# Four places for the routed rows, their loads behind ScalarE's copies, the row weight on y, and copies on POOL

## The reference

```python
masked_scores = sg.reshape(T, E)
_, selected_experts = jax.lax.top_k(masked_scores, K)
weights = jnp.take_along_axis(original_scores, selected_experts, axis=-1)
weights = weights / jnp.sum(weights, axis=-1, keepdims=True)
...
g = jax.lax.ragged_dot(xs, w_gate, group_sizes)     # xs: rows sorted by expert
u = jax.lax.ragged_dot(xs, w_up, group_sizes)
d = jax.lax.ragged_dot(jax.nn.silu(g) * u, w_down, group_sizes)
unsort_idx = jnp.argsort(sort_idx)
out = d[unsort_idx].reshape(T, K, H)
expert_out = jnp.sum(out * weights[..., None], axis=1)
shared = jax.nn.silu(x @ sw_gate) * (x @ sw_up) @ sw_down
return (expert_out + shared).reshape(B, S, H)
```

## Time and profile before

| | us |
|---|---|
| median of 3 runs | 2272.18 |
| lowest, highest | 2271.74, 2274.15 |
| the profiled execution | 2276.63 |
| its span, first to last instruction | 2274.9 |

### The profile page before, as it was taken

How to read it: one execution, slowest core, us unless ns; L and a number is a source line. 1 busy time by engine, 2 the same in 40 slices (tenths; PEclk the granted TensorE clock), 3 DMA queues, 4 the chain that set the end, 5 groups by cost and what they waited for, 6 DMA issues and landing times. The chain is left out here.

```text
span 2274.9 us, 34385 instructions
## 1 busy us (share of the span) xinstructions
PE 1932.6 (85%) x10056; PEld 1382.9 (61%) x10057; DVE 1309.4 (58%) x2357; ACT 573.1 (25%) x1164; POOL 1119.3 (49%) x552
## 2 busy tenths in 40 slices
PE   5956887868887589998799999999999999997891
PEld 3423443743333233343499988888888888886781
DVE  2564543556776767775674446666666666654540
ACT  3320222401114244453222212222222222221210
POOL 0000000002557365664035567666667788877886
PEclk8977998898996789999899999999999999998996
DMA  3043101402224456721125445556555656654999
GB/s 117 0 118 100 52 22 32 172 18 88 80 87 160 153 195 224 233 69 44 40 82 180 180 139 169 160 170 174 159 157 153 196 160 189 193 156 129 209 210 212
DMA packets 272640, 306.01 MB, mean 135 GB/s; under 512 B 40857, under 2 KB 184217, under 8 KB 272569
## 3 DMA queue, kind: packets, MB, share of 16 engines
q1 hardware_dynamic: 142776, 187.24, 25.6%
q10 hardware_dynamic: 108288, 66.88, 11.1%
q0 software_dynamic: 21504, 50.93, 9.5%
HBM read 186.42 MB, written 118.55 MB: 134 GB/s over the span
## 5 line engine op out<-in xcount | busy, mean ns | idle before, releaser
L2495 PE MATMUL psum<-e_gu_high,e_rowT_high 128*128 (+1 forms) x1272 | 435.0, 344 | 43.9 <-issue 19.9
L2495 PE MATMUL psum<-e_gu_low,e_rowT_high 128*128 (+1 forms) x1272 | 410.5, 324 | 0.0
L2495 PEld LDWEIGHTS psum<-e_gu_high,e_rowT_high 128*128 128x128 f32 x1272 | 241.5, 190 | 88.8 <-issue 86.4
L2295 DVE TENSOR_TENSOR e_midT_low<-psum,e_midT_high 128x256 fp32r<-128x256 f32 x159 | 67.5, 424 | 348.8 <-ACT e_midT_high L2209 326.9
L2500 PE MATMUL psum<-e_gu_high,e_rowT_low 128*128 (+1 forms) x1272 | 257.7, 325 | 0.0
L2495 PEld LDWEIGHTS psum<-e_gu_low,e_rowT_high 128*128 128x128 f32 x1272 | 242.6, 191 | 2.2
L2203 ACT CAST e_rowT_high<-psum 128x512 fp32r<-128x512 f32 x127 | 74.6, 587 | 596.4 <-issue 407.9
L2500 PEld LDWEIGHTS psum<-e_gu_high,e_rowT_low 128*128 128x128 f32 x1272 | 215.2, 190 | 0.0
L2515 PE MATMUL psum<-e_d_high,e_midT_high 128*128 (+3 forms) x477 | 190.7, 400 | 3.6 <-ACT e_midT_high L2209 2.4
L2515 PE MATMUL psum<-e_d_low,e_midT_high 128*128 (+3 forms) x477 | 188.3, 395 | 0.0
L2119 POOL TENSOR_TENSOR e_gu_high<-f_gu_in,e_ones 128x1408 fp32r<-128x1408 f32 x31 | 78.6, 2535 | 182.1 <-PE psum L2500 161.4
(11 more groups left out here) (381 smaller groups left out, 3941.3 us busy)
## 6 DMA issues: line engine op xcount, KB each, us to landing
d_sorted<-f_hs SPq DMA_DIRECT2D x32, 1048.0 KB, 10.3
d_y<-f_arena ACTq DMA_DIRECT2D x127, 256.0 KB
e_row<-d_sorted ACTq DMA_DIRECT2D x500, 64.0 KB
f_gu_in<-in_L_ffn_w_gate SPq DMA_DIRECT2D x32, 704.0 KB
f_gu_in<-in_L_ffn_w_up SPq DMA_DIRECT2D x32, 704.0 KB, 6.1
f_d_in<-in_L_ffn_w_down SPq DMA_DIRECT2D x32, 512.0 KB
d_y<-f_hs SPq DMA_DIRECT2D x8, 1024.0 KB, 5.7
f_d_in<-in_L_ffn_w_down SPq DMA_DIRECT2D x32, 192.0 KB
```

Source lines behind the costliest of these rows:

```text
L2495: nc.tensor.matmul(bank[:, 0:M].unsqueeze(1), rowT_high[par][:, k, :], w[:, bass.ds(buffer, 1), k, at:at + M], start=(k == 0 and n == 0), ...
```

## The change

There are four places for routed rows instead of two, and they lie in the first four tiles of `hs`, which are free once their rows have been scattered and turned. SP fills four places before the loop. ScalarE issues the loads of tile i+4 after `copy_midT`, ahead of the store of y, behind waits for the pick and the transpose of tile i. On DVE the transpose of tile i+1 moves from the end of step i-1 to the start of step i, behind the copy of y; rowT's low part then comes ahead of midT's; the pick for tile i moves from step i-1 to the place behind the product of tile i; the product no longer takes the row weight; y is multiplied by it on its way out of PSUM. The loops of ScalarE and DVE hold four tiles instead of two; PE's program stays as it is. On POOL the four products with ones become `tensor_copy`.

```diff
-        row = [sbuf(nc, stack, f"e_row{n}", [P, D]) for n in range(2)]
-        side = [sbuf(nc, stack, f"e_side{n}", [P, 2 * TOPK]) for n in range(2)]
+        row = [hs[:, n, 0:D] for n in range(ROWS)]
+        side = [hs[:, n, D:ROW] for n in range(ROWS)]
         picked = [sbuf(nc, stack, f"e_picked{n}", [P, TOPK]) for n in range(2)]
-        row_weight = [sbuf(nc, stack, f"e_row_weight{n}", [P, 1]) for n in range(2)]
+        row_weight = [sbuf(nc, stack, f"e_row_weight{n}", [P, 1]) for n in range(ROWS)]
...
+        QUAD_END = (TILES - 1 - ROWS) // ROWS
+        def load_row(eng, tile, place):
 
             for r in range(P // BLOCK):
-                eng.dma_start(row[par][r * BLOCK:(r + 1) * BLOCK, :].rearrange("b (n q) -> b n q", n=P // BLOCK).unsqueeze(1),
-                              sorted_blocks[:, tile, :, r * P:(r + 1) * P]).then_inc(row_loaded[par], 16)
-            eng.dma_start(side[par][:].unsqueeze(1), sorted_tiles[:, tile, D:ROW]).then_inc(row_loaded[par], 16)
+                eng.dma_start(row[place][r * BLOCK:(r + 1) * BLOCK, :].rearrange("b (n q) -> b n q", n=P // BLOCK).unsqueeze(1),
+                              sorted_blocks[:, tile, :, r * P:(r + 1) * P]).then_inc(row_loaded[place], 16)
+            eng.dma_start(side[place].unsqueeze(1), sorted_tiles[:, tile, D:ROW]).then_inc(row_loaded[place], 16)
 
...
-            for par in range(2):
-                load_row(sp, slice(par, par + 1), par)
+            sp.wait_ge(row_turned, NT + ROWS)
+            for n in range(ROWS):
+                load_row(sp, slice(n, n + 1), n)
...
-                nc.gpsimd.tensor_tensor(d_high[:, par, 0:2, :], d_in[:, 0:2, :], ones[:, 0:1].unsqueeze(2).broadcast_to((P, 2, D)), ALU.mult)
-                nc.gpsimd.tensor_tensor(d_high[0:LAST_M, par, 2, :], d_in[0:LAST_M, 2, :], ones[0:LAST_M, 0:1].broadcast_to((LAST_M, D)), ALU.mult).then_inc(high_ready, 1)
+                nc.gpsimd.tensor_copy(d_high[:, par, 0:2, :], d_in[:, 0:2, :])
+                nc.gpsimd.tensor_copy(d_high[0:LAST_M, par, 2, :], d_in[0:LAST_M, 2, :]).then_inc(high_ready, 1)
...
-                nc.gpsimd.tensor_tensor(gu_high[:, par, :, 0:M], gu_in[:, :, 0:M], ones[:, 0:1].unsqueeze(2).broadcast_to((P, CC, M)), ALU.mult).then_inc(high_ready, 1)
+                nc.gpsimd.tensor_copy(gu_high[:, par, :, 0:M], gu_in[:, :, 0:M]).then_inc(high_ready, 1)
...
-                nc.gpsimd.tensor_tensor(gu_high[:, par, :, M:2 * M], gu_in[:, :, M:2 * M], ones[:, 0:1].unsqueeze(2).broadcast_to((P, CC, M)), ALU.mult).then_inc(high_ready, 1)
+                nc.gpsimd.tensor_copy(gu_high[:, par, :, M:2 * M], gu_in[:, :, M:2 * M]).then_inc(high_ready, 1)
...
-            def load(i, par):
+            def load(i, place):
                 act.wait_ge(weight_taken, i - SHARED_TILES + 1)
                 act.wait_ge(blocks_turned, i - SHARED_TILES + 1)
-                load_row(act, bass.ds(i + 2 - SHARED_TILES, 1), par)
+                load_row(act, bass.ds(i + ROWS - SHARED_TILES, 1), place)
 
...
-            def steps(i, par, loads=False, stores=False, old=True, more=True, blocks=True):
-                if loads:
-                    load(i, par)
-                if more and blocks:
-                    copy_blocks(i + 1, 1 - par)
+            def steps(i, par, old=True, more=True):
                 silus(i, par)
                 if old:
                     copy_midT(i - 1)
-                if more and not blocks:
+                if more:
                     copy_rowT(i + 1, 1 - par)
+            def routed_steps(i, place, fills, loads=True, stores=True, more=True):
+                par = place % 2
+                if more:
+                    copy_blocks(i + 1, 1 - par)
+                silus(i, par)
+                copy_midT(i - 1)
+                if loads:
+                    load(i, place)
                 if stores:
                     store(i - 2, par)
 
...
-            for i in range(SHARED_TILES, SHARED_TILES + 2):
-                steps(i, i % 2, loads=True)
-            with act.Fori(SHARED_TILES // 2 + 1, LOOP_END) as n:
-                for par in range(2):
-                    steps(n * 2 + par, par, loads=True, stores=True)
-            for i in range(LOOP_END * 2, TILES):
-                steps(i, i % 2, loads=(i + 2 < TILES), stores=True, more=(i + 1 < TILES))
+            for i in range(SHARED_TILES, SHARED_TILES + ROWS):
+                routed_steps(i, i % ROWS, (i + 1 - SHARED_TILES) // ROWS + 1, stores=(i >= SHARED_TILES + 2))
+            with act.Fori(SHARED_TILES // ROWS + 1, QUAD_END) as n:
+                for q in range(ROWS):
+                    routed_steps(n * ROWS + q, q, n + ((q + 1) // ROWS + 1 - SHARED_TILES // ROWS))
+            for i in range(QUAD_END * ROWS, TILES):
+                routed_steps(i, i % ROWS, (i + 1 - SHARED_TILES) // ROWS + 1, loads=(i + ROWS < TILES), more=(i + 1 < TILES))
...
-            def turn_blocks(i, par, loads):
+            def turn_blocks(i, place, loads):
                 dve.wait_ge(rowT_low_ready, i)
-                dve.wait_ge(row_loaded[par], LANDED * loads)
+                dve.wait_ge(row_loaded[place], LANDED * loads)
                 nc.vector.transpose(XT.rearrange("p (n k b) -> p n k b", k=CC, b=BLOCK),
-                                    row[par][:].rearrange("p (n b k) -> p n k b", k=CC, b=BLOCK)).then_inc(blocks_turned, 1)
+                                    row[place].rearrange("p (n b k) -> p n k b", k=CC, b=BLOCK)).then_inc(blocks_turned, 1)
 
...
-            def take_weight(i, par):
+            def take_weight(i, place):
 
                 expert = tile_expert[:, bass.ds(i - SHARED_TILES, 1)]
-                nc.vector.scalar_tensor_tensor(picked[par][:], side[par][:, TOPK:2 * TOPK], expert, side[par][:, 0:TOPK],
-                                               ALU.is_equal, ALU.mult, accum_out=row_weight[par][:]).then_inc(weight_taken, 1)
+                nc.vector.scalar_tensor_tensor(picked[place % 2][:], side[place][:, TOPK:2 * TOPK], expert, side[place][:, 0:TOPK],
+                                               ALU.is_equal, ALU.mult, accum_out=row_weight[place][:]).then_inc(weight_taken, 1)
 
...
-            def multiply(i, par, taken=None):
+            def multiply(i, par):
                 dve.wait_ge(silu_ready, i + 1)
                 dve.wait_ge(up_done, i + 1)
-                if taken is None:
-                    nc.vector.tensor_tensor(mid[par][:], silu[par][:], U[par][:, 0:M], ALU.mult).then_inc(mid_ready, 1)
-                else:
-                    dve.wait_ge(weight_taken, taken)
-                    nc.vector.scalar_tensor_tensor(mid[par][:], silu[par][:], row_weight[par][:], U[par][:, 0:M],
-                                                   ALU.mult, ALU.mult).then_inc(mid_ready, 1)
-
-            def copy_y(i, par, stored=None):
+                nc.vector.tensor_tensor(mid[par][:], silu[par][:], U[par][:, 0:M], ALU.mult).then_inc(mid_ready, 1)
+            def copy_y(i, place, stored=None):
+                par = place % 2
                 dve.wait_ge(down_done, i + 1)
+                dve.wait_ge(weight_taken, i - SHARED_TILES + 1)
                 if stored is not None:
 
                     dve.wait_ge(y_stored[par], stored)
-                nc.vector.tensor_copy(y[par][:], Y[par]).then_inc(y_copied, 1)
+                nc.vector.tensor_scalar(y[par][:], Y[par], row_weight[place][:], None, ALU.mult).then_inc(y_copied, 1)
 
...
-            def routed_steps(i, par, more=True, loads=None):
+            def routed_steps(i, place, fills, more=True):
+                par = place % 2
+                if more:
+                    turn_blocks(i + 1, (place + 1) % ROWS, fills)
+                    low_blocks(i + 1, 1 - par)
                 low_midT(i - 1)
-                if more:
-                    low_blocks(i + 1, 1 - par)
-                    take_weight(i + 1, 1 - par)
-                multiply(i, par, i - SHARED_TILES + 1)
-                if loads is not None:
-                    turn_blocks(i + 2, par, loads)
+                multiply(i, par)
+                take_weight(i, place)
 
...
-            take_weight(SHARED_TILES, 0)
-            turn_blocks(SHARED_TILES + 1, 1, 1)
-            routed_steps(SHARED_TILES, 0, loads=2)
+            routed_steps(SHARED_TILES, 0, 1)
             add_y(SHARED_TILES - 1, 1)
-            for i in range(SHARED_TILES + 1, SHARED_TILES + 4):
-                routed_steps(i, i % 2, loads=(i - SHARED_TILES) // 2 + 2)
-                copy_y(i - 1, (i - 1) % 2, 16 if i == SHARED_TILES + 3 else None)
-            with dve.Fori(SHARED_TILES // 2 + 2, LOOP_END) as n:
-                for par in range(2):
-                    routed_steps(n * 2 + par, par, loads=n - SHARED_TILES // 2 + 2)
-                    copy_y(n * 2 + par - 1, 1 - par, 16 * (n - SHARED_TILES // 2 - 1 + par))
-            for i in range(LOOP_END * 2, TILES):
```

(13 more changed lines are left out.)

14 lines of the change are left out of this document (7 added, 7 removed).

## The result

| kernel | time, us (median; lowest to highest) | span of the profiled execution, us |
|---|---|---|
| before | 2273.16 (2271.74 to 2275.50) | 2274.9 |
| after | 2310.48 (2310.15 to 2310.84) | 2308.9 |

The ratio after to before is 1.0157, 95% interval 1.0145 to 1.0169: the change makes the kernel slower by 1.6%. The profiled execution of after took 2310.68 us. The forecast was 2294 us: the direction is right, and 2310.5 lies inside the likeliest case's own range (2277 to 2312), near its upper end.

What follows compares the result with a forecast made beforehand. PE's routed stage was taken as nearly a matmul stream, losing when another engine is late. Loop +31, first routed tile -2.8, end -9.8 and +3 made +21.4 on 2276.63, 2298.0; less 4.45 for the median, 2294 us, range 2250 to 2335.

Steps and rivals of the forecast that it cites:

- likeliest case: The forecaster's own case, a slower kernel at 2294 us, range 2277 to 2312; chance 0.46.
- nearly equal bounds of 2.01 and 2.03: ScalarE's cast: earliest start in us of a tile, 2.01 by the load issues behind a free pick, 2.03 by the turn.
- The loop: Routed tiles up to POOL's first gather: about +1.0 to +1.2 us per split, times 27 splits, +31 us.
- two worked cases: Four tiles over two splits: 27.82 us with the split in an odd tile (26.69 before), 27.44 in an even one (26.6).
- The undisturbed pair: Two loop tiles without a waiting pick: 6.35 us even plus 6.79 odd, 13.14 together, 6.57 per tile.
- T + 3.05: ScalarE's next cast can't start before the pick's end T plus 0.17, 2.43 and 0.45 us for loads and store.
- POOL's copies: On POOL, copies replacing 2.5 us products take 1.3 us for 1408 elements; a whole split gets 3.7 us shorter.
- (b): Rival: POOL copies no faster than products, +1.95 us a split, +53 in the loop, 2325 us; chance 0.22.
- First routed tile: The turn comes before the pick, so PE's down product starts at 1351.1 instead of 1353.90: -2.8 us.
- The end: POOL's chain from first gather to PE's waiting gate: -9.8 us; afterwards, with PE and POOL level, +3 us.
- (a): Rival: the move is a gain, the pick's wait stays off the path or ScalarE isn't held; 2255 us, chance 0.25.
- (c): Rival: picks mostly wait behind only one low part, excess near 0.65 us per split, gains cancel it; 2272 us, chance 0.07.

Runs made afterwards that it cites:

- fastest kernel: Changed kernel with the turn at the end of DVE's step, loads of the tile before, PE's loop of four and the pick's weights read from PSUM: 2232.7 us.
- pick from PSUM: Changed kernel, but DVE first copies the row's six weights to PSUM and the pick reads them there: 2276.8 us.
- turn at the end: Changed kernel with the transpose back behind the pick at the end of DVE's step, one tile further ahead: 2311.8 us.
- later loads: Changed kernel, but ScalarE's step issues the loads that hang on the pick of the tile before: 2267.3 us.
- products back: Changed kernel with POOL's four products by ones put back in place of the copies: 2382.2 us.
- copies only: Kernel before with POOL's four products by ones replaced by copies, nothing else: 2292.5 us.
- body of four tiles: Changed kernel with the loads of the tile before and PE's loop body holding four tiles instead of two: 2260.9 us.
- products and later loads: Changed kernel with POOL's products by ones put back and with the loads of the tile before: 2298.2 us.

## Why the prediction was right, and which of its terms were off

**The mechanism stands.** Of the signs named ahead, these are in the rows: load issues near 5.4 us of a tile, odd tiles lengthened with the copy at 3.30, a pick that waits over 1.5 us and a tile over 8 us behind it where a split starts in an odd tile, copies near 1.3 us, PE's idle time at "issue". One failed: the cast does come before 2.0, at 1.37, in the even tile that follows a long one, since the long tile gives the engines behind PE their slack back; and behind the 14 even splits the held tile is 7.6 to 7.85, not over 8, as it is behind the 13 odd ones (8.2 to 8.7). The mechanism is more than an argument now: taking the loads from behind the current pick gave back 43 of the loop's 47 us, and taking only the turn away gave nothing, as the nearly equal bounds of 2.01 and 2.03 had it. The ring of four places and the bodies of four on ScalarE and DVE were not tried alone; the fastest kernel keeps both.

**The number.** The forecast was +21.4 us and 2294; the spans of the two profiled executions differ by 34.0, and the median is 2310.5. Of the 17 us of the miss, 12.6 lie in the stretches below. The other 4.3 are no part of the mechanism: the forecast took 4.45 us off for the way from the profiled execution to the median, and in after that way is 0.2. The loop's term alone was short by 16 us, and the other stretches gave 3.4 back. The forecast did not need two large errors to cancel, but it met its own range by only 1.5 us.

**The loop, +31 forecast, +47.0 measured, over 27 splits in both.** The mean tile is 7.13 us where I had expected 6.9 to 7.0. First the sum itself: the two worked cases, 27.82 and 27.44 us, lie 1.54 and 1.16 above four undisturbed tiles (4 x 6.57 = 26.28). Their mean of 1.35, times 27, gives +29 against the 638 us of before; "+1.0 to +1.2 per split" does not follow from 27.44 against 26.6, which is 0.84. Then two terms were too small.

The undisturbed pair. I had 6.35 and 6.79, mean 6.57; it is 6.38 and 6.97, mean 6.675. Over 96 tiles that is 10 of the 16 us. The step that failed is the cast at 2.03: it is at 2.20. I had put y's scaling at "0 to 0.1 us and take 0". Y's write starts 0.40 into the odd tile (1494.60 - 1494.20), not 0.30, and holds DVE for 0.67 (to 1495.27), not 0.59; from the turn to the cast it is 1.13 (to 1496.40), against 1.14. Together that is the missing 0.17. The bounds of the term contained each half, but I placed it on a path without slack and still wrote zero. What makes y start later was not tried. The kernel with the pick from PSUM keeps y's operand and its waits and starts it 0.32 into such a tile (1490.79 - 1490.47), so these alone do not explain the 0.40.

The split. The excess over undisturbed tiles is (698.8 - 98 x 6.675) / 27 = 1.65 us; mine was (638 + 31 - 96 x 6.57) / 27 = 1.42. That is the other 6 us. The term is "T + 3.05": the held cast comes 3.43 us after its pick (1507.89 to 1511.32), since four load issues took 2.08 us there and 1.81 in a free tile; even behind a free pick it is 3.28 (1494.88 to 1498.16 in the kernel with the turn at the end), and mostly 3.16 or 3.28 in that kernel. In an even split the four tiles from 1572.49 on are 6.38, 7.75, 7.29 and 6.63 = 28.05 against 27.44; in others the third one is held longer (from 1842.14 on 6.35, 7.66, 7.80 and 6.65 = 28.46).

**POOL's copies, 1.3 forecast.** All 31 of the first copy, a group of the view by line and shape:

```profile
L2123 POOL CAST e_gu_high<-f_gu_in 128x1408 fp32r<-128x1408 f32 x31 | 42.2, 1361 | 323.8 <-PE psum L2505 301.9 <-DMA X<-d_y,f_slots 17.3 <-issue 4.7
...
L2111 POOL CAST e_d_high<-f_d_in 128x1024 fp32r<-128x1024 f32 x31 | 32.3, 1043 | 5.6 <-PE psum L2525 5.0
```

1.36 us: the fill of the earlier trace rows was the right neighbour, and rival (b) is out. The Trainium skill (GPSIMD Engine Reference, "Elementwise — side-by-side cycle accounting") led to an estimate of 1.21 us; the trace is 0.15 above it, and the measurement decides.

**First routed tile, -2.8 forecast, -1.3 measured.** The turn does come first and no pick stands in the way. But after 2.76 us in which PE stood idle the gate product runs at a granted clock of 0.66 in the mean of 4 us, and 0.50 (1.2 GHz, the lower level) from 1346 to 1348, where its matmuls take 0.49 us instead of 0.32. The down product starts 5.85 us behind the gate (1350.62 - 1344.77) where I had 4.3. Before, the same slow stretch (0.66 from 1346 to 1350) lay beneath the pick's wait, which ended later; the prediction took that wait away and put nothing in its place for the clock.

**The end, -9.8 forecast.** First gather to the waiting gate: 68.03 against 78.17, so -10.1. The term was right, as it counted POOL's own instructions on a chain that was POOL's. With what follows it the stretch gives -11.6 + 1.9 = -9.7 against -9.8 + 3 = -6.8; what I had allowed for two engines that "run level" there was 3 us too much.

**Rivals.** (a), the pick's wait off the path, decided at an excess of 0.65 us per split; it is 1.65. A small excess is what the later loads bring about: an excess of (655.4 - 98 x 6.675) / 27 = 0.05 us, and 2267 us. (b), whose copies would have been as slow as the products, was under-priced by half (+53, and +108 in the kernel with the products back). (c) did not occur.

## What to carry to other kernels

Before an engine's queue gets a wait for a small instruction elsewhere, ask what is queued behind the wait and whether the small instruction can be held; issuing what hangs on the previous iteration's event instead, at the same place and cost, was worth 43 us here. Where two paths end together, an experiment must take away both, and a forecast may not put a term on either at zero. Speeding up an engine that is off the path can cost time by phase alone (18 us here): find what it holds, and take that away (one operand into PSUM), before making it faster.

## What the runs showed of the hardware that I had not expected

A DVE instruction that reads two inputs from SBUF waits for the end of the POOL instruction that is running, even for six elements: up to 3.29 us for 0.22 us of work. Less than 0.1 us before that end it waited for the whole of the next one (products back). Where its output goes doesn't matter (mean 822 ns into PSUM, 830 into SBUF); with one input in PSUM it never waits (mean 222 ns; in the last kernel all 127 took 220 to 223). The Trainium skill (SBUF — State Buffer, "Who interferes with whom") says that a DVE instruction with two SBUF inputs contends with a GpSimd instruction that reads SBUF, and that one with at most one such input, outside its two-port modes, does not; the traces agree, with these numbers.

Four load issues on ScalarE's queue took 1.81 us in a tile without a wait. Behind the 26 picks of after's loop that waited over 1.5 us they took 2.07 to 2.09, and in the kernel with the copies only too. It is not the wait as such: before, 26 picks waited as long, and the issues behind them took 1.82 or 1.83. Why is open.

The way from the midT copy over the jump back of PE's loop to the next gate is not always 3.67 us. With a body of four tiles it is at most 3.69 in 17 of the 25 tiles that end at the jump, and 3.77 to 3.96 in the eight held ones. With a body of two there are such tiles too: 3.93 us (7.66 - 3.73) in the tile at 1566.41 of the kernel with products and later loads. So a longer body is not shown to make the jump dearer, and the cause is open.
